# A third pre1b slot, the FFN one step later, and the attention transposes ahead of the second layer norm

## The reference

```python
q, k, v = x @ Wq + bq, x @ Wk + bk, x @ Wv + bv       # 16, 2 and 2 heads of 64
scores = einsum('bgrsd,bgswd->bgrsw', qg, k_win)      # keys s-128 .. s+127
out = einsum('bgrsw,bgswd->bgrsd', softmax(scores), v_win)
x = layernorm(x + out @ Wo + bo)
# ffn: W_real, W_imag are 512 x 512, built from small tensors G1, G2
out_real = x_real @ W_real.T - x_imag @ W_imag.T + bias_real
out_imag = x_real @ W_imag.T + x_imag @ W_real.T + bias_imag
x = layernorm(x + concatenate([out_real, out_imag]))
```

## Time and profile before

| | us |
|---|---|
| median of 2 runs | 1664.53 (1663.73 to 1665.33) |
| the profiled execution | 1669.48 |
| span of its slowest core (core 3) | 1667.9 |
| spans of its cores | 1637.1 to 1667.9 |
| PE busy | 938.3 (56%) |
| DVE busy | 521.2 (31%) |
| ACT busy | 394.0 (24%) |
| POOL busy | 324.1 (19%) |

### The profile page before, as it was taken

One profiled execution on the slowest core, in us unless ns is written; L12 is line 12 of the kernel. 1 busy time (PEld: TensorE's weight loads), 2 busy tenths in 40 slices (PEclk: granted clock), 3 DMA queues, 4 the chain that ended last, 5 costly groups with the idle time before them and its releaser, 6 DMA issues.

```text
span 1667.9 us, 17855 instructions; the slowest of 8 cores (1637.1 to 1667.9 us)
## 1 busy us (share of the span) xinstructions
PE 938.3 (56%) x4712; PEld 368.9 (22%) x4712; DVE 521.2 (31%) x1764; ACT 394.0 (24%) x675; POOL 324.1 (19%) x324
## 2 busy tenths in 40 slices
PE   0184337655666646665553765665766566566653
PEld 0031002222222222222221322221322222222221
DVE  0002432343133332433432003333134313333343
ACT  3332123222322222222201242222322222222200
POOL 0000013222132211332210032222122212222210
PEclk9986556666776667767666776666766677666656
DMA  5500000000100010000002000001000010000000
GB/s 143 170 26 1 1 0 1 13 13 26 51 13 14 14 63 4 23 13 14 13 26 80 35 0 1 26 13 39 26 14 13 13 63 14 14 13 14 13 13 26
DMA packets 15874, 44.57 MB, mean 27 GB/s; under 512 B 3091, under 2 KB 5539, under 8 KB 15782
## 3 DMA queue, kind: packets, MB, share of 16 engines
q0 software_dynamic: 9216, 33.56, 5.5%
q1 hardware_dynamic: 6566, 9.87, 2.1%
HBM read 26.65 MB, written 16.78 MB: 26 GB/s over the span
## 4 chain that ended last, share of the span: by engine, by line
PE 49%; DVE 23%; issue 12%; DMA 7%; ACT 6%; DVEq 1%; POOL 1%; SPq 0%; ACTq 0%; POOLq 0%
PE pW L816 12%; PE pW L666 10%; PE pW L440 8%; DVE attn L619 5%; PE pS L534 5%; DVE scr L679 4%; PE pS L591 4%; DMA xs<-x 4%; DVE pre L838 2%; ACT EX L552 2%; PE pW L820 2%; PE pW L670 1%; DVE attnT L649 1%; DVE Rrec L609 1%; DVE pre1b L713 1%
## 5 line engine op out<-in xcount | busy, mean ns | idle before, releaser
L552 ACT ACTIVATE EX<-pS,expbias 128x512 bf16<-128x512 f32 x384 | 241.8, 680 | 428.4 <-PE pS L534 428.2
L666 PE MATMUL pW<-wo_sb,attnT 128*128 128x512 bf16 x512 | 182.3, 521 | 183.0 <-DVE attnT L649 183.0
L568 POOL TENSOR_TENSOR EX<-EX,maskl_s 128x512 bf16<-128x512 bf16 x128 | 143.3, 1150 | 401.2 <-ACT EX L552 400.9
L568 POOL TENSOR_TENSOR EX<-EX,maskr_s 128x512 bf16<-128x512 bf16 x128 | 144.7, 1153 | 113.4 <-ACT EX L552 112.8
L534 PE MATMUL pS<-QT,KT 64*128 64x512 bf16 x384 | 120.3, 501 | 78.9 <-ACT EX L552 77.2
L892 POOL DMA_DIRECT2D y<-outst x32 | 19.0, 592 | 656.0 <-DVE outst L884 614.5
L609 DVE RECIPROCAL Rrec<-pS 128x4 f32<-128x4 f32 x128 | 22.7, 178 | 366.7 <-PE pS L591 366.0
L440 PE MATMUL pW<-XT,wq_sb 128*128 128x512 bf16 x512 | 126.2, 413 | 8.9 <-DVE XT L420 8.9
L591 PE MATMUL pS<-VB,EX 128*128 128x65 bf16 x1536 | 83.6, 214 | 74.4 <-DVE attn L619 62.9
L666 PEld LDWEIGHTS pW<-wo_sb,attnT 128*128 128x128 bf16 x512 | 57.9, 123 | 284.5 <-issue 267.5
L816 PE MATMUL pW<-wrt,x1T 128*128 128x512 bf16 x256 | 108.7, 572 | 17.4 <-DVE Rrec L609 13.8
(11 more groups left out here) (104 smaller groups left out, 954.1 us busy)
## 6 DMA issues: line engine op xcount, KB each, us to landing
xs<-x POOLq DMA_DIRECT2D x32, 512.0 KB, 4.6
y<-outst POOLq DMA_DIRECT2D x32, 512.0 KB, 3.0
wstage<-wq SPq DMA_DIRECT2D x4, 512.0 KB, 4.3
xs<-wq SPq DMA_DIRECT2D x4, 512.0 KB, 4.3
wstage<-wo SPq DMA_DIRECT2D x4, 512.0 KB, 4.2
xs<-wo SPq DMA_DIRECT2D x4, 512.0 KB, 4.2
wstage<-wk SPq DMA_DIRECT2D x1, 512.0 KB, 4.7
xs<-wv SPq DMA_DIRECT2D x1, 512.0 KB, 4.6
```

Of the source, the lines that this page charges most:

```text
L552: i = sca.activation(EX[:, exi * 512:(exi + 1) * 512], pS[quad % 2][:, :], AF.Exp, bias=expbias[:])
L568: i = gps.tensor_mul(EX[:, exi * 512:(exi + 1) * 512], EX[:, exi * 512:(exi + 1) * 512], m[:]) \
L666: ten.matmul(pW[half][:, :], attnT[:, ring * 1024 + c * 128: ring * 1024 + (c + 1) * 128], wo_sb[:, c * 1024 + half * 512: c * 1024 + (hal ...
```

## The change

pre1b gets a third slot, used by block number modulo 3, while all other rings stay at two. The loop gets one more turn, and a fourth block is at work in it: Q3 = k-3. x1t, the FFN and ln2out are called for Q3 and no longer for Q2, so one step later than before; statT stays at Q2, so it now runs one step ahead of the FFN that reads its row. Inside a step: av 1 moves up to follow scores 0,1; normalise 0, 1 follows FFN half 0; av 2 moves up to follow scores 1,0; av 3 with normalise 2, 3 follows scores 1,1; attnT follows at once, ahead of scores 2,0; and ln2out moves from in front of scores 2,0 to behind them, directly ahead of wo half 0. No instruction is of another kind or shape.

```diff
-    pre1b = sb("pre1b", [128, 2 * 1024], BF16)
+    pre1b = sb("pre1b", [128, 3 * 1024], BF16)
...
         def ln1_unit(b, S):
             ring = S % 2
+            p3 = S % 3
             slot = S % 8
             c0 = ring * 8
-            rx1 = E.res(f"x1{ring}")
+            rx1 = E.res(f"x1{p3}")
...
-                    pre1b[:, ring * 1024 + half * 512: ring * 1024 + (half + 1) * 512],
+                    pre1b[:, p3 * 1024 + half * 512: p3 * 1024 + (half + 1) * 512],
...
         def x1t_unit(b, S):
             ring = S % 2
+            p3 = S % 3
             rpt = E.res("pT")
             rxt = E.res(f"x1T{ring}")
-            rx1 = E.res(f"x1{ring}")
+            rx1 = E.res(f"x1{p3}")
...
-                                  pre1b[:, ring * 1024 + c * 128: ring * 1024 + (c + 1) * 128],
+                                  pre1b[:, p3 * 1024 + c * 128: p3 * 1024 + (c + 1) * 128],
...
-            for k in range(18):
-                S, P, Q2 = k, k - 1, k - 2
+            for k in range(19):
+                S, P, Q2, Q3 = k, k - 1, k - 2, k - 3
                 if S < 16:
                     sc_unit(b, S, 0, 0)
                     exp_unit(b, S, 0, 0)
-                if 0 <= Q2 < 16:
-                    x1t_unit(b, Q2)
+                if 0 <= Q3 < 16:
+                    x1t_unit(b, Q3)
                 if 0 <= P < 16:
                     av_unit(b, P, 0)
                 if S < 16:
@@ -921,37 +924,41 @@
                     exp_unit(b, S, 0, 1)
                     mask_unit(b, S, 0, 0)
                     mask_unit(b, S, 0, 1)
+                if 0 <= P < 16:
+                    av_unit(b, P, 1)
                 if 0 <= Q2 < 16:
                     statT_unit(b, Q2)
-                    ffn_unit(b, Q2, 0)
+                if 0 <= Q3 < 16:
+                    ffn_unit(b, Q3, 0)
+                if 0 <= P < 16:
+                    recip_unit(b, P, 0)
+                    recip_unit(b, P, 1)
+                    normts_unit(b, P, 0)
+                    normts_unit(b, P, 1)
                 if S < 16:
                     sc_unit(b, S, 1, 0)
                     exp_unit(b, S, 1, 0)
-                if 0 <= Q2 < 16:
-                    ffn_unit(b, Q2, 1)
+                if 0 <= P < 16:
+                    av_unit(b, P, 2)
+                if 0 <= Q3 < 16:
+                    ffn_unit(b, Q3, 1)
                 if S < 16:
                     sc_unit(b, S, 1, 1)
                     exp_unit(b, S, 1, 1)
                 if 0 <= P < 16:
-                    av_unit(b, P, 1)
-                    recip_unit(b, P, 0)
-                    recip_unit(b, P, 1)
-                    normts_unit(b, P, 0)
-                    normts_unit(b, P, 1)
-                    av_unit(b, P, 2)
                     av_unit(b, P, 3)
                     recip_unit(b, P, 2)
                     recip_unit(b, P, 3)
                     normts_unit(b, P, 2)
                     normts_unit(b, P, 3)
-                if 0 <= Q2 < 16:
-                    ln2out_unit(b, Q2)
+                    attnT_unit(b, P)
                 if S < 16:
                     sc_unit(b, S, 2, 0)
                     exp_unit(b, S, 2, 0)
                     mask_unit(b, S, 2, 0)
+                if 0 <= Q3 < 16:
+                    ln2out_unit(b, Q3)
                 if 0 <= P < 16:
-                    attnT_unit(b, P)
                     wo_unit(b, P, 0)
                 if S < 16:
                     sc_unit(b, S, 2, 1)
```

More of the change, by code:

```diff
@@ L722, in ln1_unit @@
             rx1["r"] = ev_add
-            ev_var = lnstats(st1, c0, lambda: pre1b[:, ring * 1024:(ring + 1) * 1024], EPS)
+            ev_var = lnstats(st1, c0, lambda: pre1b[:, p3 * 1024:(p3 + 1) * 1024], EPS)
             E.ev[f"var1_{ring}"] = ev_var
```

## The result

The changed kernel takes 1477.65 us (median; 1471.1 to 1491.91), the kernel before in the same series 1664.27. The ratio is 0.891, 95% interval 0.887 to 0.896: faster. The forecast was 1463 us, range 1390 to 1565. The chip also has a slower state, in which the cores of a die show a lower granted clock; ratios and intervals are of executions outside it, while a median in us can include one of them. The profiled execution took 1483.83 us; core 7, the slowest, has a span of 1482.0 us at a mean granted clock of 0.709, where the earlier trace rows have 0.687.

A forecast was written before the change was run, and what follows sets the result against it. The prediction took PE's in-order chain with its DVE round trips as the bound. Terms 213 + 15 + 4.5 - 30.2 gave 202 us off 1669.5, so 1467.5, and 5 less for the median: 1463 us, range 1390 to 1565.

The forecast's parts named there:

- (a): Last av unit to wo: attnT ahead of ln2out cuts 9.45 us to 5.3, 4.2 us less a step.
- (b): Av units moved up: waits of 1.94 and 0.31 us go, 2.25 us a step; delayed POOL masks cost nothing.
- (c): Third pre1b slot, FFN one step later: 0.6 us less between first score matmul and FFN, per step.
- (d): Extra last turn, k=18: last wo to end grows from 35.9 to 51.0 us, 30.2 more for both sequences.
- The clock: PE's granted clock: the sum leaves it as it is, keeping today's share of full rate.
- the partly risen clock: Rival: wo's second half, second FFN half and units behind it at 2.4 GHz, step 28.2 us, 1427 us; chance 0.18.
- bound of the clock: Plain step's two limits: 32.8 us with all at 1.2 GHz, 23.8 us with all at 2.4 GHz.
- The second bound: Plain step of 23.8 us, all at 2.4 GHz; by the skill, removing the 5.97 us pause would bring it.
- The slower rival: wo waits for all of ln2out_unit: 5.8 us return each step, 1625 us, or 1725 at lower clock; chance 0.07.
- the one by which the waits only move to the turn: Rival: the change does nothing, waits moving to the step's turn, where PE idles about 2.4 us; no separate chance.

The follow-up runs named there:

- e1: Kernel before with only attnT moved ahead of scores 2,0 and ln2out behind them: 1601.52 us, ratio 0.968.
- e9: Changed kernel with ln2out back ahead of scores 2,0 and attnT back behind them: 1541.61 us, ratio 0.926.
- e7: Changed kernel without the two POOL masks behind the y store (block 2, pair 1), so part of the computation is left out: 1417.86 us, ratio 0.853.
- e11: Changed kernel with y store behind mask 2,1, rstd1 and ln1 statistics in the next step, statT behind FFN half 1, av 2 normalised earlier: 1425.76 us, ratio 0.859.
- e8: Changed kernel with the av units and their normalisation back together behind scores 1,1: 1540.35 us, ratio 0.928.
- e2: Kernel before with only av 1, av 2 and the normalisation of 0 and 1 moved as in the change: 1544.08 us, ratio 0.932.
- e5: Changed kernel without the third pre1b slot and the extra turn, new inner order kept: 1472.3 us, ratio 0.887.
- e4: Changed kernel with the y store issued on POOL behind mask 2,1 in place of ahead of it: 1428.75 us, ratio 0.863.

## Why the prediction was right, step by step

The time fell into the range and on the forecast side, 15 us or 1% above the predicted one. The mechanism, PE's chain and its DVE round trips, is what the runs show; the closeness is partly luck, since two missing terms of opposite sign stand behind it.

**(a)** The chain from av to wo came out as summed: 2.48 us from the end of av 3 (1336.19) to the transposes (1338.67), then 2.64 to wo (1341.31), 5.1 in place of the 5.3 forecast. What failed is the term's value, 4.2 us a step or 125 us: it was worth 56 (e1) to 58 (e9). The failing sentence stands in (b): I asked only who waits for POOL's masks and priced their delay at nothing, and never what runs beside them. Every DVE duration was taken as unchanged. The squares took 51 us longer in all. e7, which takes the meeting away, gains 0.891 - 0.853 = 3.8%, 63 us, 2.2 a step; part of that is PE's busy time, which is lower there too (887.0 us against 910.0). In e1 the squares take 55 us longer and PE is busy for 13 us more; 125 less both is 57, and 56 were measured. The Trainium skill (SBUF — State Buffer, Who interferes with whom) says that a DVE instruction with two SBUF inputs contends with a GpSimd instruction that reads SBUF, and that the one that issues later is blocked by the other. The traces agree that the two hold each other up, with 1.23 us alone, 3.21 beside two masks and 3.05 for a single column. They don't agree on the length: DVE was held beyond the mask that had started first, to the end of the run of masks, and in e11 by masks that started after it. I had not brought the rule to the prediction. It speaks against the change, and the kernel before shows how near the two were: the masks ended at 1125.00, 0.55 us before the squares began.

**(b)** 2.25 us a step, 72 us: 61 inside the change (e8), 113 alone (e2), of which 74 are waits.

**(c)** Worth nothing together with (d), as summed, inside the change (e5 against the changed kernel). The FFN follows statT with no wait (1356.79 above). The step k=2 without the FFN took 23.7 and 22.6 us for about 22 forecast.

**(d)** From the last wo to the end 49.8 us, forecast 51.0. Outside the steps and the last turn 7.0 us were added, where the sum had 15.1 for the first sequence's last turn less 4.5 for step k=1, 10.6.

**The clock** was kept at its share. It rose, 0.687 to 0.709 in the profiled executions, and the same matmuls cost PE 28 us less in the run (938.3 to 910.0). The steps were summed at 213 + 15 = 228 us less and came to 206.8: 228 less the 51 us of longer squares and with the 28 of PE's busy time is 205. Without the masks' hold the ratio is 0.853, 1420 us, and my sum of 1463 would have been 43 us too high; PE is busy there for 51 us less than before. So the bookkeeping fits, but the clock has not been changed by itself, and its share is argued, not shown. Of the rivals, the partly risen clock (1427) is the one that the kernel came near to once the masks were out of the way. Neither bound of the clock, 32.8 and 23.8 us a step, was met: the plain steps are 29.8 in the mean, and 27.2 without the masks' hold. The second bound was also what taking the long pause away was said to bring; e1 takes it away, and the clock there is no higher.

**The slower rival**, wo waiting for the whole of `ln2out_unit`, fell: the wait is 1.1 us. So did the one by which the waits only move to the turn, in part: PE's idle time there went from 0.81 + 2.42 us to 5.56 in one piece, 2.3 more, but through the squares, which it did not name.

The plain step was forecast at 29.5 us and said to lie between 28 and 31: 29.8 in the mean, 30.7 in the one shown. PE waits for masks in three places of the run, 1.5 us in all; it was DVE that was held by them.

## What to carry to other kernels

When a reordering moves work on DVE or POOL, list what now runs beside it and whether both read SBUF, as carefully as who waits for whom: moving one store behind two masks on POOL gave 47 us here, a quarter of what the whole change gave. A part's value alone is not its value in the sum (the depth: about 2% alone, nothing inside; the av units: 113 us alone, 61 inside), so measure both before crediting it. One step is a poor measure where steps differ: take sums over the run. And a forecast that lands within 1% may still hold two wrong terms; single-part runs find them.

## What was unexpected of the hardware

- A DVE instruction with two SBUF inputs can be held by a run of POOL masks until the last of the run: 3.2 us beside two masks, 5.7 beside four, 1.23 alone; on one column 3.05 us in place of 0.16. It isn't always so, and it holds POOL too. The squares of `ln2out_unit`, started 0.66 us after the first of two masks (1341.88 above), took only 1.57 us, and the two masks 3.24 in place of 2.26; the longest single mask of that kernel took 2.14 us, 1.17 before:

```profile
L568 POOL TENSOR_TENSOR EX<-EX,maskr_s x128: 1148/1155/2137, 251.6 to 1411.2; 128x512 bf16<-128x512 bf16 x128
```

  The adds of `ln2out_unit`, which read one input from PSUM, kept their 0.68 and 0.69 us in the same place. What decides whether DVE comes between two masks or waits for all of them, no run here shows.
- Plain steps gather at few lengths in some kernels: near 37.4 and 34.1 us before, 30.7 after, 26.6 to 27.3 for most in e4 and e7. In e5 most lie between 28 and 32, in e11 between 23 and 30. Taking 2.0 us off the chain moved one step by 4.0 (e7), with the granted clock going from 0.67 to 0.76 in it, but the mean step by 2.6. So a microsecond on the chain can be worth more than itself in a step, and no run here tells ahead when.
